# Rounding the triangle on GpSimd into two buffers, a shorter splitting of the exponents, rounded right sides on VectorE, and a new order of steps on all engines

## What is computed

```python
mixed = silu(causal_conv4(x @ Wqkv.T + bqkv))      # 8 heads of q and k, 16 heads of v, 128 channels each
beta, g = sigmoid(x @ Wb.T + bb), -exp(A_log) * softplus(x @ Wa.T + ba + dt_bias)
q, k = l2norm(q) * 128**-0.5, l2norm(k)
def step(state, q_t, k_t, v_t, g_t, b_t):           # per head, over all tokens
    state = state * exp(g_t)
    delta = (v_t - k_t @ state) * b_t
    state = state + outer(k_t, delta)
    return state, q_t @ state
core = rmsnorm(core) * norm_w * silu(x @ Wz.T + bz)
x = x + layernorm(core @ Wout.T + bout)
x = x + layernorm(shared_expert(x) + routed_experts(x, top 8 of 16))   # both on layernorm(x)
```

## Time and profile before

| | us |
|---|---|
| median of 3 runs | 3316.34 (3315.38 to 3320.57) |
| the profiled execution, whole | 3309.96 |
| its span, first to last instruction | 3308.2 |
| PE busy | 3040.9 (92%) |
| DVE busy | 2625.7 (79%) |
| ACT busy | 2457.3 (74%) |
| POOL busy | 2275.8 (69%) |

### The profile page before, as it was taken

The page is one execution under the profiler, slowest core; times in us unless marked ns, Lnnn a source line. Parts: engine busy times, 40 slices in busy tenths (PEclk is TensorE's granted clock), DMA queues, the critical chain, the costliest instruction groups (busy, mean ns, idle before and its releaser), DMA issues.

```text
span 3308.2 us, 74142 instructions
## 1 busy us (share of the span) xinstructions
PE 3040.9 (92%) x22560; PEld 2722.1 (82%) x22688; DVE 2625.7 (79%) x8462; ACT 2457.3 (74%) x5922; POOL 2275.8 (69%) x5380
## 2 busy tenths in 40 slices
PE   4999999999999999999999999999999999999996
PEld 3888888888888888888888888888888888888885
DVE  4788888888888888787878888888888878878874
ACT  3777777777777777777777777777787777787772
POOL 3777777767777777676767777777777767777670
PEclk8999999999999999999999999999999999999996
DMA  5111111111111111111111111111111111111110
GB/s 185 37 46 37 39 48 35 45 42 37 44 43 35 46 42 37 39 48 35 38 44 42 38 36 48 39 39 46 39 36 48 39 37 46 41 35 48 39 35 12
DMA packets 424102, 144.57 MB, mean 44 GB/s; under 512 B 211168, under 2 KB 421664, under 8 KB 423200
## 3 DMA queue, kind: packets, MB, share of 16 engines
q1 hardware_dynamic: 423712, 139.83, 16.1%
HBM read 93.11 MB, written 46.66 MB: 42 GB/s over the span
## 4 chain that ended last, share of the span: by engine, by line
POOL 38%; PE 22%; issue 17%; DMA 12%; ACT 7%; DVE 3%; POOLq 0%; SPq 0%; ACTq 0%; DVEq 0%
POOL Tp L1576 12%; POOL Tp L1583 8%; DMA DL<-Ln 7%; DMA Cb<-DL 5%; POOL Ln L1470 3%; ACT L839 3%; POOL Tp L1573 3%; PE bB L643 2%; POOL Tm L1585 2%; POOL Yb L1585 2%; POOL Yb L1600 2%; PE bF L475 2%; PE bX L522 2%; PE bQ L530 1%; PE bB L715 1%
## 5 line engine op out<-in xcount | busy, mean ns | idle before, releaser
L1148 DVE SCALAR_TENSOR_TENSOR Y<-bF,Cv,Y 128x127 f32<-128x127 f32 (+2 forms) x3072 | 853.3, 339 | 149.6 <-ACT Y L856 139.4
L475 PE MATMUL bF<-XnT,Wqkv 128*128 128x128 f32 x4096 | 561.0, 281 | 0.0
L475 PEld LDWEIGHTS bF<-XnT,Wqkv 128*128 128x128 f32 x4096 | 521.7, 194 | 13.5 <-issue 2.1
L928 ACT ACTIVATE XiT<-bXT 128x512 fp32r<-128x512 f32 x256 | 153.0, 598 | 436.2 <-PE bXT L559 436.2
L856 ACT ACTIVATE Y<-bF,Cv 128x128 f32<-128x128 f32 x1024 | 384.1, 458 | 77.7 <-PE bF L475 77.7
L1583 POOL TENSOR_TENSOR Tp<-Tp 32x64 f32<-32x64 f32 (+2 forms) x768 | 358.2, 466 | 60.2
L839 ACT ACT_TABLE_LOAD x257 | 329.7, 1283 | 5.3 <-PEq L1668 0.7
L1576 POOL TENSOR_TENSOR Tp<-Cb,Yb 32x64 f32<-32x64 f32 (+1 forms) x384 | 276.3, 719 | 30.1
L1576 POOL TENSOR_TENSOR Tp<-Yb,Tm 32x64 f32<-32x64 f32 (+1 forms) x384 | 275.9, 718 | 30.1
L572 PE MATMUL bX<-Xi,Qi 128*128 128x128 f32 x1536 | 285.1, 309 | 0.8 <-DVE Qi L1190 0.8
L1530 POOL TENSOR_TENSOR Ln<-Ln,Cf 128x512 f32<-128x512 f32 x128 | 163.8, 1280 | 173.8 <-DMA DL<-Ln 173.8
(11 more groups left out here) (228 smaller groups left out, 8645.1 us busy)
## 6 DMA issues: line engine op xcount, KB each, us to landing
DL<-Ln SPq DMA_DIRECT2D x128, 256.0 KB, 2.2
XiT<-DX SPq DMA_DIRECT2D x128, 256.0 KB, 2.8
Xi<-DX SPq DMA_DIRECT2D x128, 256.0 KB, 3.2
DX<-Yb SPq DMA_DIRECT2D x256, 32.0 KB, 1.9
Xf<-x SPq DMA_DIRECT2D x32, 128.0 KB, 2.9
Wqkv<-wqkv SPq DMA_DIRECT2D x4, 1024.0 KB, 17.4
Cb<-DL SPq DMA_DIRECT2D x128, 32.0 KB, 1.9
Xr<-x SPq DMA_DIRECT2D x32, 128.0 KB, 3.1
```

Of the source, the lines that this page charges most:

```text
L475: last = mm(bank[:, i, :], Wqkv[:, k, c:c + P], XnT[:, k, :], start=(k == 0), stop=(k == KT - 1))
L1148: last = stt(y, bank[:, i, 0:P - shift], Cv[:, g * TILES + tile, n:n + 1], y, ALU.mult, ALU.add)
```

## The change

It has four parts.

1. POOL's new `rounded_l` computes `Ln - identity` straight into `LnR` in fp32r, between `attention` and `minus_one`, from the triangle in `Ln`. `LnR` has two buffers, by the group's parity. ACT's copy is gone. `minus_one` stands behind it.
2. `exponents` on POOL splits into three bf16 parts with one instruction less, and the sum that only ACT's `scales` needs comes last.
3. `rounded_r`, the fp32r copy of the right sides, is done by DVE (`tensor_copy`) right behind `right_side`, not by ACT.
4. `Hn` shares the buffer `Xn`, with other semaphores for it, and the order of steps in `item` is new on PE, ACT, DVE, POOL and SP.

```diff
-        HGf = sb("HGf", [P, 2, 2 * GH])
+        HGf = sb("HGf", [P, 2 * GH])
-        LnR = sb("LnR", [P, GH, P], F32R)
+        LnR = sb("LnR", [P, 2, GH, P], F32R)
-        Hn = sb("Hn", [P, HID])
...
                 if "f" in stages:
                     triangle_out(f)
                     blocks_in(f)
+                if g == 0 and "c" in stages and not first:
+                    next_in(t)
+                if g == 1 and "s" in stages:
+                    tokens_in(t)
+                if g == GROUPS - 1 and "e" in stages:
+                    tokens_out(t - 1)
+                if "f" in stages:
                     inverses_out(f)
                     inverses_in(f)
-                if g == GROUPS - 1 and "e" in stages:
-                    tokens_out(t - 1)
-                if g == 1 and "s" in stages:
-                    tokens_in(t)
...
-            def rounded_l(f):
-                act.wait_ge(sem["lni_done"], at("lni_done", f))
-                act.wait_ge(sem["q_full"], at("q_full", ahead(f, -1), LEVELS))
-                op(LnR[:, :, :], Ln[:, live(f), :, :], ACT.Copy).then_inc(sem["lnr_done"], 1)
...
-                op(Rr[:, :, :], R[:, :, :], ACT.Copy).then_inc(sem["rr_done"], 1)
...
+            def rounded_r(w):
+                dve.wait_ge(sem["r_done"], at("r_done", w))
+                nc.vector.tensor_copy(Rr[:, :, :], R[:, :, :]).then_inc(sem["rr_done"], 1)
...
                 tt(Parts[:, 0:n], HG[:, 0:n], one, ALU.mult).then_inc(sem["parts_done"], 1)
+                pool.wait_ge(sem["parts_done"], at("parts_done", f, 1))
+                tt(Parts[:, n:2 * n], HG[:, 0:n], Parts[:, 0:n], ALU.subtract).then_inc(sem["parts_done"], 1)
+                tt(HGf[:, :], HG[:, 0:n], Parts[:, 0:n], ALU.subtract).then_inc(sem["parts_done"], 1)
+                pool.wait_ge(sem["parts_done"], at("parts_done", f, 3))
+                tt(Parts[:, 2 * n:3 * n], HGf[:, :], Parts[:, n:2 * n], ALU.subtract).then_inc(sem["parts_done"], 1)
                 tt(HG[:, 2 * GH:3 * GH], HG[:, GH:2 * GH], HG[:, 3 * GH:4 * GH], ALU.add).then_inc(sem["hg_done"], 1)
...
+            def rounded_l(f):
+                pool.wait_ge(sem["neg_done"], at("neg_done", f))
+                pool.wait_ge(sem["q_full"], at("q_full", ahead(f, -2)))
+                tt(LnR[:, f[1] % 2, :, :], Ln[:, live(f), :, :], ident.unsqueeze(1).to_broadcast([P, GH, P]), ALU.subtract)\
+                    .then_inc(sem["lnr_done"], 1)
...
             def minus_one(f):
-                pool.wait_ge(sem["neg_done"], at("neg_done", f))
+                pool.wait_ge(sem["lnr_done"], at("lnr_done", f))
                 pool.wait_ge(sem["ln_out"], at("ln_out", f))
...
+                if state:
+                    decay_keys(w)
                 if new:
                     before_first(a)
-                if state:
-                    decay_keys(w)
                 if front:
                     minus_l(f)
                     attention(f)
+                    rounded_l(f)
                     minus_one(f)
                     base_inverse(f)
```

194 lines of the change are left out of this document (89 added, 105 removed).

## The result

The changed kernel took **3369.98 us** in the median of 4 runs (3355.19 to 3378.14), the kernel before 3315.86 (3304.66 to 3320.57). The ratio is 1.016, with an interval of 1.012 to 1.021: slower by 54 us, where 80 us of gain were forecast. The range ended at 3322.

The account below looks back on a forecast made before the run. PE was taken to bound the kernel, with only its 5.96 us idle per chunk to win; terms summed to -2.58 us per chunk, times 31 -80 us, forecasting 3236 us (3204 to 3298), range 3200 to 3322.

Parts of the forecast that it names:

- L516, -1.48 of 1.48: PE's parts_t wait for POOL's last exponent part: all 1.48 us per chunk would go.
- L510, -1.1 of 1.40: PE's ktr wait for DVE's sum of squares: 1.1 of 1.40 us per chunk would go.
- L530, -0.7 of 0.82: Exponents' product on PE waiting for ACT's PartsT and its issue: 0.7 of 0.82 us per chunk would go.
- L559, -0.4 of 1.39: PE's invert_xt wait for DVE's mask: starting ahead of left_over saves 0.4 us per chunk; the mask's own 0.68 stays.
- L732, +0.5: New wait of PE's laT for la at g = 3: +0.5 us per chunk, between 0.1 and 0.7.
- SP's queue, +0.3: On SP, tokens_out ahead of inverses_out delays the read of Xi: +0.3 us per chunk (0 to 0.9).
- Unseen waits, +0.3 (0 to 1.5): Waits not followed, xnT for its norm and the next qs for update_s: +0.3 us per chunk.
- The copies at 0: Triangle on POOL (1.28 us) and right sides on DVE (0.43 us) priced at 0, as covered by waits or distance.
- The clock, no term: PE's clock was taken as 0.99 of full speed already, so the sum had no term for it.
- the gaps only move: Rival: PE's removed waits come back elsewhere; two thirds of 4.1 us returning gives -0.3 per chunk, 3308 us; chance 0.10.
- The prediction's price, 1.25 us in each of four items: Rival: DVE and POOL lock each other out, holding back L559's mask: +2.4 us per chunk, 3391, typically 3340; chance 0.12.

Follow-up runs that it names:

- n: Kernel before with one swap on DVE, the mask mask_q(v, 0) ahead of left_over: 3310.83 us, ratio 0.999.
- q: Changed kernel with five identity multiplications on PE ahead of its wait for the mask at L559, in the item with g = 0: 3313.46 us.
- j: Changed kernel with both copies (triangle and right sides) on ACT again, new order and shorter splitting kept: 3412.15 us.
- a: Changed kernel with SP's tokens_out behind inverses_in again: 3377.16 us, ratio 1.019.
- r: Kernel before with triangle on POOL, shorter splitting, right sides on DVE, sum of squares first (PE, DVE, ACT) and mask ahead of left_over: 3273.27 us.
- b: Changed kernel with the copy of the right sides back on ACT, behind query_state: 3457.14 us, ratio 1.043.
- c: Changed kernel with the rounded triangle written by ACT again: 3375.54 us, ratio 1.018.
- g: Kernel before with only the rounded triangle moved to POOL, into a double buffer, all orders kept: 3290.37 us, ratio 0.992.
- i: Kernel before with only the copy of the right sides moved from ACT to DVE: 3297.50 us, ratio 0.996.
- k: Kernel before, old order on all five engines, with triangle on POOL, shorter splitting and right sides on DVE together: 3290.74 us, ratio 0.992.
- t: Kernel before with three identity multiplications on PE ahead of its wait for the mask at L559, item with g = 0: 3289.63 us.
- o: Changed kernel with the exponents' parts back in their old place on PE and ACT: 3351.49 us, ratio 1.010.
- m: Kernel before with vtr and parts_t ahead of solve, core_t behind it on PE; parts_t and solved ahead of core_t on ACT: 3435.95 us.

## Why the prediction was wrong

By its own steps, per chunk:

- **L516, -1.48 of 1.48:** right, 35.5 to 3.2 us in 2400.
- **L510, -1.1 of 1.40:** right, and more: 33.7 to 4.5, 1.2 per chunk.
- **L530, -0.7 of 0.82:** wrong twice. The row was nearly all the lost record of L528 (0.376 us of work four times a chunk), which no order takes away: `n`, which has the record, waits 0.3 us in 2400 there. And a real wait for ACT's `PartsT` came, since PE asks for it earlier: 14.7 us in the changed trace, which lacks the record, and 9.6 and 17.8 in `q` and `j`, which have it.
- **L559, -0.4 of 1.39:** the swap is worth that by itself (`n`), but L559 rose by 0.6 in the whole change. **This is the step that failed**: "with g = 0 nothing stands between" was said of the mask's own time, and I kept the arrival of PE where it was. PE, relieved at L516 and L510, came to L559 somewhat earlier; DVE came to the mask a little later. An item of the commoner kind, on PE and on DVE, and one row of POOL:

```profile
2344.04 0.63 PE L547 MATMUL bQ<-XiT,LnR 128*128 128x128 f32 x4
2346.43 0.66 PE L559 MATMUL bXT<-Qi,Xi 128*128 128x128 f32 x4 [1.75 <-DVE Qi L1178]
```
```profile
2336.87 0.43 DVE L1357 TENSOR_TENSOR Yo<-Yo,X 128x256 f32<-128x256 f32 x1
...
2338.64 0.43 DVE L1199 CAST Rr<-R 128x512 fp32r<-128x512 f32 x1
2338.98 1.92 DVE L1234 SCALAR_TENSOR_TENSOR O<-O,Fr,Gz 128x128 f32<-128x128 f32 x4
...
2341.57 3.41 DVE L1136 SCALAR_TENSOR_TENSOR Y<-bF,Cv,Y 128x127 f32<-128x127 f32 x12
...
2345.08 0.60 DVE L1160 TENSOR_TENSOR Y<-Y,Hd 128x12 f32<-128x12 f32 x1
2345.60 0.68 DVE L1178 TENSOR_TENSOR Qi<-bQ,Cf 128x512 fp32r<-128x512 f32 x1
...
2339.34 1.15 POOL L1532 TENSOR_TENSOR Kd<-Kn,Sc 128x512 f32<-128x512 f32 x1
```

  From the end of `Yo` to the mask it is 8.3 us (2337.30 to 2345.60), and was 8.15 before (1579.95 to 1588.10), though `left_over` no longer stands ahead of it. PE starts the product L547 6.9 us behind the end of `Yo`, in the median of the items with g = 0, and did so at 7.1 before. I followed each wait's own releaser and not the whole queue of DVE. That queue, from `Yo` to the mask with g = 0, in the mean: the copy adds 0.43 us, `gated` 0.73 (1.39 to 2.12), `first_tokens` 0.25 (0.35 to 0.60); `left_over` takes away 0.67 and idle time 0.59. In the six items of the other kind (the timeline of the result) DVE is done, and the mask waits for the late product of L547.
- **L732, +0.5:** right, 11.0 us in 2400, 0.46.
- **SP's queue, +0.3:** the wait was there (L547, +0.42), but taking it away gave nothing (`a`).
- **Unseen waits, +0.3 (0 to 1.5):** L715 0.78, L728 0.53, L632 +0.2: +1.5, at the end of its bounds.
- **The copies at 0:** the durations were right, the worth was not: alone they gain 24 and 17 us, perhaps through a shorter ACT. And DVE's copy is not covered on the way to the mask, as the 0.43 us above show.
- **The clock, no term:** +2.07. I had read its mean, 0.99, as "nothing to lose". In the trace before, the half level already took 0.85 us per chunk; it answered to the gaps of PE. Where L559 waited 1.24 us, it now waits 1.4 to 1.9 us in one piece, or L547 waits 1.2 to 1.6 us and L559 0.88 just behind it, and the half level comes in 19 of 23 chunks, not in 8 of 24.

Of the rivals, "the gaps only move" was right in kind: the idle time of PE stayed, 6.00 to 6.27. It had 0.10, and no price for the clock. (Its sum is off as well: the terms taken away are 3.68 us, not 4.1, so it comes to -0.13 per chunk and 3312 by its own rule.)

DVE's operations with two inputs do get longer beside POOL's, as the Trainium skill, "SBUF — State Buffer", "Who interferes with whom" says, and the rows agree: `first_tokens` takes 475 ns in the mean, 309 before. The prediction's price, 1.25 us in each of four items, was not found. But its place was partly right: it named `gated` beside `decay_keys`. In the changed kernel POOL does `decay_keys` (L1532) ahead of `before_first`, and in 23 of 24 items with g = 0 one of the four instructions of `gated` takes 1.13 us beside it, where 0.34 is usual; in the kernel before and in `r` none does. `b`, `c` and `j` all keep POOL's order, and `gated` takes 2.15 to 2.17 us in them. With `first_tokens` this puts 0.98 us into DVE's queue ahead of the mask, in one item of four. What it costs the kernel is not shown: no run puts POOL's order back in the changed kernel.

Shown by runs: the loss is in the order (`j`), not in the copies (`g`, `i`, `k`), not in SP's queue (`a`), and most of it is clock that a filled gap gives back (`q`, `t`). Not settled: how much of the order's loss each place carries, and how much of it comes through DVE's longer operations. The parts' third costs 121 us alone and 19 within the change, the rest of the order (`o` against `r`) 78, and `q` removes 57 with the order as it is, so the costs of the places do not add up.

## What to carry over

When PE is nearly full, take a wait away only if the engine that releases its *next* wait comes earlier too; else the time is gathered into one longer gap. Price such a gap twice: its own length, and the work at half clock behind it, read from windows just after PE's gaps. Where a gap must stay, a few multiplications into a bank that is overwritten next can be worth more than a better order. Try the parts of a new order one by one: here the copies, priced at nothing, gained, and the order, priced at 80 us, lost.

## What the runs showed of the hardware

- PE's clock fell to 1.2 GHz behind gaps of 2.38 us in one piece (`m`), 1.75 us in one piece and 1.44 + 0.88 us with one short group between (changed kernel), and in one window stayed there through 6.7 us in which PE was busy without a gap. Not every gap of such a length was followed by it: 19 of 23 items with g = 0 in the changed kernel, and in the kernel before 4 of the 19 in which L559's 1.24 us was the only wait near.
- Five multiplications in the gap (1.33 us) kept it at 2.4 GHz: 4.60 us per item with g = 0 at the lower level went to 0.00. Three in the kernel before brought 1.56 us there to 0.71.
- The same matmuls took 3.72 us at the lower level and 1.94 at the upper.
- One instruction of DVE with two inputs in SBUF (`gated`, 128 columns) took 1.13 us beside one of POOL (`decay_keys`, 1.15 us), and 0.34 us otherwise.
- A missing matmul record reads as idle time and as a wait with no releaser ("issue") of the line behind it: count a line's multiplications against its weight loads before a wait is priced.
